# A sixteen-head attention pipeline: VectorE scales the contexts of an older unit ahead of the row maximum of the same step

## Chip, cores and metric

The kernel runs on one core of one Trainium2 chip. The metric is the device time in microseconds. Lines such as L1484 are lines of the kernel before. The engines are called TensorE (PE; PEld for its weight loads), VectorE (DVE), ScalarE (ACT), GpSimd (POOL) and SyncE (SP).

## What is computed

Twelve residual blocks on eight sequences of 256 tokens with 128 features. Three of them hold the attention that the change touches: one causal attention (block L1) and two mixtures of two attentions (block L3), all with 16 heads of 8 features. Cut to that:

```
def _L1_attn_ref(x, w_qkv, b_qkv, w_out, b_out):          # causal, 16 heads of 8
    qkv = jnp.einsum('btc,cd->btd', x, w_qkv) + b_qkv
    ...
    scores = jnp.einsum('bhqd,bhkd->bhqk', q, k) * scale
    scores = jnp.where(causal, scores, jnp.finfo(scores.dtype).min)
    attn = jax.nn.softmax(scores, axis=-1)
    out = jnp.einsum('bhqk,bhkd->bhqd', attn, v)
    return jnp.einsum('btc,cd->btd', out, w_out) + b_out

def _L3_ffn_ref(...):                                     # M = 2 attentions, mixed by mha_probs
    scores = jnp.einsum('mbhtk,mbhsk->mbhts', q, kk) / jnp.sqrt(jnp.float32(KD))
    attn = jax.nn.softmax(scores, axis=-1)
    ctx = jnp.einsum('mbhts,mbhsk->mbthk', attn, v)
    mha_out = jnp.einsum('mbthk,mhkd->mbtd', ctx, mha_wo) + mha_bo[:, None, None, :]
    x = x + jnp.einsum('mbtd,bm->btd', mha_out, mha_probs)
    ...

x = x + _L1_attn_ref(_layernorm(x, axis=-1), ...)
...
x = x + 0.5 * _L3_ffn_ref(x, ...)
x = x + _L3_attn_ref(x, ...)
x = x + 0.5 * _L3_ffn_ref(x, ...)
```

## The kernel before

Each engine has its own program, and the programs meet only in semaphores. The class SmallHeads is the pipeline of a sixteen-head attention. Its unit of work is one sequence with one set of weights: 8 units in the causal attention (the subclass L1Attend), 16 in each of the two L3 attentions (two sets of weights for each of eight sequences).

All engines walk the same list of steps, 16 to a unit: step i of unit k scores head i of unit k. Older units are further on in the same steps, so that one pass of 16 steps works on several units at once. For unit k, the one being scored:

- TensorE writes the scores of a head into one of three banks (`score_bank`, banks 0, 1 and 5 in turn), so the scores of step s wait for the row maximum of step s-3 (`topped`, `s - 2`).
- VectorE takes the row maximum of the scores (L1484; in the causal attention L1482, two masked halves with an accumulator read each) and raises `topped`.
- At step 0 GpSimd splits the 16 maxima of unit k-1 into bf16 parts (L1522 to L1528, `mx_split`) and then the projections of unit k+2 (L1536 to L1543, as long as there is a unit k+2). At step 3 TensorE turns the parts of the maxima (`mx_turned`), ScalarE copies them and SyncE sends them to the rows beside q.
- At odd steps TensorE scores a pair of heads of an older unit anew, with the maximum subtracted in the product, and ScalarE takes the exponentials (L1455). In the causal attention GpSimd then clears what lies above the diagonal (L1515, `selected`).
- Every fourth step is a quad: TensorE multiplies the exponentials of four heads with the values, which carry a column of ones, so that contexts and row sums come out together in bank 6. For w counted in quads, the causal attention waits for the select of pair 2w+1. At step 8 of unit k that is the pair scored at step 3.
- Unit k-3 is finished in bank 7, which five operations share in turn: at step 5 TensorE turns the raw contexts (L1351, `turned`), VectorE takes the reciprocal of the row sums (L1490) and scales the contexts (L1493, `scaled`). At step 7 TensorE writes the value projection of unit k into the same bank, so it waits for `scaled`, and ScalarE copies the values (L1667, L2237, `v_copied`). At step 9 TensorE turns the scaled contexts (L1365), for which it waits for `v_copied`, and ScalarE copies these (L1671, L2242).

TensorE's program has, in step 5, the four transposes L1351 first and the scores of step 5 behind them. The steps go on after the last unit has been scored, so units k-3 are scaled for k = 3 to units+2.

Of the kernel before, what the change touches and what calls it, by code (L numbers as in the profile page):

```python
# [9 lines left out]
ALU = mybir.AluOpType  # L10
# [3 lines left out]
P = 128  # L14
# [17 lines left out]
HEADS, KD = 16, P // 16  # L32
# [1173 lines left out]
class SmallHeads(Stage):  # L1206
# [264 lines left out]
    def heads_vector(self, eng, ch):  # L1471
        ps, V = self.k.ps, self.k.nc.vector
        for s, k, i in self.steps():
            if self.is_unit(k):
                self.wait_ge(eng, self.scored, s + 1)
                if i == 0:
                    self.wait_ge(eng, self.mx_split, k - 1)
                at = self.PAIRS * (i % 2) + i // 2
                mx = self.mx[k % 2][:, :, at:at + 1]
                if self.causal:  # L1480
                    for t, (st, end) in enumerate(((0, P), (P, 3 * P))):
                        o = V.tensor_tensor_reduce(self.masked[:, s % 3, st:end], ps[:, self.score_bank(s), st:end], self.k.mask_q[:, st:end], 1.0, MASKED, ALU.add, ALU.max, mx[:, t])  # L1482
                else:
                    o = V.tensor_reduce(mx, ps[:, self.score_bank(s), :].rearrange("p (t s) -> p t s", t=2), AXX, ALU.max)  # L1484
                o.then_inc(self.topped.sem, 1)
            u = k - 3
            if i == 5 and self.is_unit(u):
                self.wait_ge(eng, self.turned, u + 1)
                rows = ps[:, 7, :].rearrange("p (a d) -> p a d", d=32)[:, :, 0:2 * (KD + 1)].rearrange("p a (j d) -> p a j d", j=2)
                ch.did(V.reciprocal(self.rinv, rows[:, :, :, KD]))  # L1490
                ch.wait_ge()
                self.wait_ge(eng, self.turned_again, u)
                V.tensor_tensor(self.ctx.rearrange("p (a j d) -> p a j d", j=2, d=KD), rows[:, :, :, 0:KD],  # L1493
                                self.rinv.unsqueeze(3).to_broadcast([P, HEADS, 2, KD]), ALU.mult).then_inc(self.scaled.sem, 1)
            if i == 11 and self.ends_batch(u):
                self.wait_ge(eng, self.summed, u // self.members + 1)
                self.out_vector(u // self.members)
            c = self.norm_at(s, self.NORM_FINISHES)
            if c is not None:
                self.wait_overlaid(eng)  # L1500
                self.next.norm.finish(eng, ch, c)
# [1151 lines left out]
```

## Time and profile before

| | |
|---|---|
| median of 3 runs | 2002.47 us (1995.29 to 2004.57) |
| profiled execution, first to last instruction | 2003.0 us |
| causal attention (8 units) | about 1000 to 1130 us |
| first L3 attention (16 units) | about 1354 to 1595 us |
| second L3 attention (16 units) | about 1710 to 1950 us |

The profiled execution is one more run; its span of 2003.0 us holds all its instructions, and the three runs lie around it. In the span TensorE is busy 1685.2 us, VectorE 1299.4, ScalarE 1153.5 and GpSimd 579.3. In the middle of an L3 attention a unit takes 13.0 us (14.1 where it ends a sequence); in the causal one 13.0.

### The profile page before, as it was taken

The page shows a single profiled execution, that of the slowest core. Times are in us where ns is not written, and L with a number is a line of the kernel's source. Part 1 is how long each engine was busy: PE and PEld are TensorE (multiplying, and loading weights), DVE is VectorE, ACT ScalarE, POOL GpSimd, SP SyncE. Part 2 cuts the span into 40 slices and gives each one's busy share as a digit, 9 for nine tenths or more (in the row PEclk, how much of TensorE's full clock was granted, in tenths as well). Part 3 has the DMA queues.
Part 4 walks back from the last instruction along what each step waited for, and adds up shares of the span by engine and source line. Part 5 has one row for each costly group of instructions (what it writes and reads, how often), then busy time and mean ns, then how long its engine had stood idle before and what let it go on. Part 6 is the DMA issues. An engine that isn't in the chain of part 4 may idle for free.

```text
span 2003.0 us, 36848 instructions
## 1 busy us (share of the span) xinstructions
PE 1685.2 (84%) x13664; PEld 884.9 (44%) x13664; DVE 1299.4 (65%) x2611; ACT 1153.5 (58%) x2711; POOL 579.3 (29%) x727
## 2 busy tenths in 40 slices
PE   6897889798898889889688884978999877899986
PEld 2555345543455435553244332324555352355535
DVE  4875577545776577744577277637788464788856
ACT  3665455544455546555356664564888735488872
POOL 2552145301554045410265103313232001333200
PEclk9999999999899999989879897996999988699997
DMA  4000000000000000000252000015544000544401
GB/s 183 17 18 7 1 17 17 12 1 1 17 12 17 1 11 18 17 1 0 46 105 52 1 1 0 0 25 101 101 94 85 17 28 16 109 97 91 94 3 63
DMA packets 55016, 75.01 MB, mean 37 GB/s; under 512 B 5748, under 2 KB 38740, under 8 KB 54328
## 3 DMA queue, kind: packets, MB, share of 16 engines
q1 hardware_dynamic: 54840, 72.66, 16.0%
q8 instruction: 111, 1.82, 0.4%
q14 instruction: 65, 0.53, 0.1%
HBM read 46.39 MB, written 16.88 MB: 32 GB/s over the span
## 4 chain that ended last, share of the span: by engine, by line
PE 62%; DVE 13%; ACT 11%; issue 7%; POOL 4%; DMA 2%; SPq 0%; DVEq 0%; POOLq 0%; ACTq 0%
PE ps L195 58%; ACT arena L631 4%; DVE arena L1484 3%; PE ps L521 2%; ACT arena L1455 2%; DVE arena L702 2%; DVE arena L746 2%; ACT arena L268 1%; ACT arena L270 1%; PE ps L616 1%; PE ps L1365 1%; DVE arena L1493 1%; DMA arena<-arena 1%; DVE arena L721 1%; DMA arena<-scratch 1%
## 5 line engine op out<-in xcount | busy, mean ns | idle before, releaser
L195 PE MATMUL ps<-arena 32*64 32x128 f32 (+10 forms) x10152 | 705.0, 316 | 88.7 <-ACT arena L1455 25.5
L195 PEld LDWEIGHTS ps<-arena 32*64 32x64 f32 (+6 forms) x10152 | 397.7, 127 | 390.3 <-issue 124.5
L1455 ACT ACTIVATE arena<-ps 128x512 f32<-128x512 f32 (+1 forms) x640 | 333.8, 576 | 79.2 <-PE ps L195 70.4
L1484 DVE TENSOR_REDUCE arena<-ps 128x2 f32<-128x512 f32 x512 | 322.6, 685 | 87.2 <-PE ps L195 85.3
L195 PE MATMUL ps<-arena,w_L0f 128*128 128x512 f32 (+3 forms) x800 | 328.2, 542 | 16.9 <-DVEq L2488 9.3
L631 ACT ACTIVATE arena<-ps,arena 128x128 f32<-128x128 f32 x512 | 226.2, 460 | 136.0 <-DVE arena L748 136.0
L195 PE MATMUL ps<-arena,const 128*128 128x512 f32 (+1 forms) x536 | 186.1, 653 | 70.9 <-DVE arena L1966 22.1
L195 PEld LDWEIGHTS ps<-arena,w_L0f 128*128 128x128 f32 (+2 forms) x800 | 142.0, 192 | 142.4 <-issue 102.8
L828 POOL TENSOR_TENSOR arena<-arena 128x512 f32<-128x512 f32 x128 | 133.0, 1045 | 244.4 <-DVE arena L726 244.4
L702 DVE TENSOR_TENSOR arena<-ps,arena 128x1024 f32<-128x1024 f32 x128 | 152.4, 1205 | 10.0 <-PE ps L195 7.3
L642 ACT ACTIVATE arena<-ps 128x512 f32<-128x512 f32 x128 | 76.8, 600 | 94.4 <-DVE arena L702 91.7
L195 PEld LDWEIGHTS ps<-arena,const 128*128 128x128 f32 (+1 forms) x536 | 59.0, 161 | 158.2 <-issue 89.8
L820 POOL TENSOR_TENSOR arena<-arena 128x512 f32<-128x512 f32 x64 | 81.4, 1271 | 160.2 <-DVE arena L702 157.2
L746 DVE TENSOR_REDUCE arena<-ps 128x8 f32<-128x1024 f32 x64 | 78.3, 1223 | 63.7 <-PE ps L195 63.4
L721 DVE COPY arena<-ps 128x512 f32<-128x512 f32 x128 | 88.3, 689 | 47.7 <-PE ps L521 47.7
L631 ACT ACTIVATION_READ_ACCUMULATOR arena<-ps,arena 128x1 f32 x512 | 106.5, 208 | 0.0
L521 PE MATMUL ps<-const,arena 128*128 128x128 f32 x512 | 79.1, 277 | 30.2 <-issue 23.2
L1482 DVE CUSTOM_DVE_ANT_0 arena<-ps,masks_b 128x128 bf16<-128x128 f32 (+1 forms) x256 | 75.0, 354 | 36.2 <-PE ps L195 35.8
L521 PEld LDWEIGHTS ps<-const,arena 128*128 128x128 f32 x512 | 57.1, 141 | 93.2 <-issue 91.3
L1522 POOL CAST arena<-arena 128x32 bf16<-128x32 f32 x40 | 8.4, 209 | 280.0 <-DVE arena L1484 275.7
L821 POOL TENSOR_TENSOR arena<-arena 128x512 f32<-128x512 f32 x64 | 83.5, 1305 | 0.0
L195 PE MATMUL ps<-residual,const 128*128 128x512 f32 x96 | 56.9, 694 | 31.4 <-DVEq L2488 17.9
(227 smaller groups left out, 2134.2 us busy)
## 6 DMA issues: line engine op xcount, KB each, us to landing
scratch<-arena SPq DMA_DIRECT2D x40, 384.0 KB, 2.8
arena<-scratch SPq DMA_DIRECT2D x80, 192.0 KB
arena<-scratch SPq DMA_DIRECT2D x80, 128.0 KB
arena<-arena SPq DMA_DIRECT2D x64, 128.0 KB, 2.3
arena<-scratch SPq DMA_DIRECT2D x80, 88.0 KB
arena<-in_experts SPq DMA_DIRECT2D x16, 256.0 KB, 4.4
w_L0f<-in_L0f SPq DMA_DIRECT2D x2, 1557.0 KB, 12.2
arena<-arena SPq DMA_DIRECT2D x80, 12.0 KB
```

The source lines that it names most:

```text
L195: return self.nc.tensor.matmul(o, lhsT, rhs, start=start, stop=stop, skip_group_check=True)
L521: o = k.nc.tensor.transpose(k.ps[:, 6, (2 * j + t) * P:(2 * j + t + 1) * P], self.prob[G % 2][:, 2 * p + j, t, :], k.K("ident"))
L631: o = S.activation(self.prob[G % 2][:, j, t, :], k.ps[:, j, t * P:(t + 1) * P], ACT.Exp, bias=self.negm[G % 2][:, at:at + 1], scale=rn[:, ...
L642: self.k.nc.scalar.activation(self.sq[i], self.k.ps[:, self.block_bank(n), :], ACT.Square).then_inc(self.squared.sem, 1)
L702: self.k.nc.vector.tensor_tensor(prod.rearrange("p t (b s) -> p t b s", b=PER), x, tab, ALU.mult).then_inc(self.rotated.sem, 1)
L721: self.k.nc.vector.tensor_copy(self.probT[q % 4].rearrange("p j t s -> p (j t s)"), self.k.ps[:, 6, :]).then_inc(self.turn_copied.sem, 1)
L746: ch.did(V.tensor_reduce(self.mx[G % 2], ps[:, 0:4, 0:SEQ].rearrange("p j (t s) -> p j t s", t=2), AXX, ALU.max))
L820: G.tensor_tensor(y[:, i, :], first[:, 0, :], second[:, 1, :], ALU.add).then_inc(self.placed.sem, 1)
L821: G.tensor_tensor(y[:, i + 1, :], second[:, 0, :], first[:, 1, :], ALU.add).then_inc(self.placed.sem, 1)
L828: self.k.nc.gpsimd.tensor_tensor(pr, pr, rinv, ALU.mult).then_inc(self.scaled.sem, 1)
L1455: S.activation(self.pt[g % 4][:, e, 0:both], ps[:, self.shifted_bank(2 * g + e), 0:both], ACT.Exp, scale=self.scale).then_inc(self.exped.s ...
L1484: o = V.tensor_reduce(mx, ps[:, self.score_bank(s), :].rearrange("p (t s) -> p t s", t=2), AXX, ALU.max)
```

## The change

In the method of VectorE's program, the block that scales unit k-3 at step 5 stands ahead of the row maximum of step 5, not behind it. Waits and operations are the same.

```
     def heads_vector(self, eng, ch):
         ps, V = self.k.ps, self.k.nc.vector
         for s, k, i in self.steps():
+            u = k - 3
+            if i == 5 and self.is_unit(u):
+                self.wait_ge(eng, self.turned, u + 1)
+                rows = ps[:, 7, :].rearrange("p (a d) -> p a d", d=32)[:, :, 0:2 * (KD + 1)].rearrange("p a (j d) -> p a j d", j=2)
+                ch.did(V.reciprocal(self.rinv, rows[:, :, :, KD]))
+                ch.wait_ge()
+                self.wait_ge(eng, self.turned_again, u)
+                V.tensor_tensor(self.ctx.rearrange("p (a j d) -> p a j d", j=2, d=KD), rows[:, :, :, 0:KD],
+                                self.rinv.unsqueeze(3).to_broadcast([P, HEADS, 2, KD]), ALU.mult).then_inc(self.scaled.sem, 1)
             if self.is_unit(k):
                 self.wait_ge(eng, self.scored, s + 1)
...
                 o.then_inc(self.topped.sem, 1)
             u = k - 3
-            if i == 5 and self.is_unit(u):
...
             if i == 11 and self.ends_batch(u):
```

VectorE's program in an L3 attention, around the scaling of one unit (k even). A row with x5 stands for five row maxima; L1490 is the reciprocal, L1493 the scaling. Before:

```order
L1484 TENSOR_REDUCE arena<-ps 128x2 [waits mx_split,scored]
L1484 TENSOR_REDUCE arena<-ps 128x2 [waits scored] x5
L1490 RECIPROCAL arena<-ps 128x32 [waits turned]
L1493 TENSOR_TENSOR arena<-ps,arena 128x256 [waits turned_again,vector_step]
L1484 TENSOR_REDUCE arena<-ps 128x2 [waits scored] x10
```

The same place in the changed kernel, where the row maximum is L1493, the reciprocal L1478 and the scaling L1481:

```order
L1493 TENSOR_REDUCE arena<-ps 128x2 [waits mx_split,scored]
L1493 TENSOR_REDUCE arena<-ps 128x2 [waits scored] x4
L1478 RECIPROCAL arena<-ps 128x32 [waits turned]
L1481 TENSOR_TENSOR arena<-ps,arena 128x256 [waits turned_again,vector_step]
L1493 TENSOR_REDUCE arena<-ps 128x2 [waits scored] x11
```

One maximum, that of step 5, has moved from ahead of the reciprocal to behind the scaling. The causal attention is the same, with four instructions to a maximum. Before:

```order
1209 L1482 ISA arena<-ps,masks_b 128x128 [waits scored]
1210 L1482 ISA arena 128x1
1211 L1482 ISA arena<-ps,masks_b 128x256
1212 L1482 ISA arena 128x1
1213 L1490 RECIPROCAL arena<-ps 128x32 [waits turned]
1214 L1493 TENSOR_TENSOR arena<-ps,arena 128x256 [waits turned_again,vector_step]
```

And in the changed kernel (maximum L1491):

```order
1209 L1478 RECIPROCAL arena<-ps 128x32 [waits turned]
1210 L1481 TENSOR_TENSOR arena<-ps,arena 128x256 [waits turned_again,vector_step]
1211 L1491 ISA arena<-ps,masks_b 128x128 [waits scored]
1212 L1491 ISA arena 128x1
1213 L1491 ISA arena<-ps,masks_b 128x256
1214 L1491 ISA arena 128x1
```

The four instructions of the maximum of step 5 now follow the scaling. The order on the other engines is unchanged.

## Rows read from the trace of the kernel before

**Rows 1.** The page, part 1: busy time, share, instructions.

```profile
PE 1685.2 (84%) x13664; PEld 884.9 (44%) x13664; DVE 1299.4 (65%) x2611; ACT 1153.5 (58%) x2711; POOL 579.3 (29%) x727
```

**Rows 2.** Who waits for the scaling, L1493: us in total, times.

```profile
L1493 DVE TENSOR_TENSOR arena<-ps,arena x40: 424/424/426, 1038.6 to 1947.1; 128x256 f32<-128x256 f32 x40
...
  PE ps L195: 15.5, 31
```

**Rows 3.** Groups, TensorE, 1390 to 1570: busy, mean ns | idle before.

```profile
L195 PE MATMUL ps<-w_L3m,arena 128*128 128x128 f32 x52 | 8.9, 293 | 4.3 <-DVE arena L1493 4.3
```

**Rows 4.** Timeline, TensorE, causal attention: start, us, what [idle before].

```profile
1049.67 0.66 PE L1351 MATMUL ps<-const,arena 128*128 128x128 f32 x4
...
1052.15 0.68 PE L195 MATMUL ps<-w_L1a,arena 128*128 128x128 f32 x4 [1.38 <-DVE arena L1493]
```

**Rows 5.** Timeline, TensorE, an L3 unit.

```profile
1453.46 0.63 PE L1351 MATMUL ps<-const,arena 128*128 128x128 f32 x4
1454.02 1.72 PE L195 MATMUL ps<-arena 48*128 48x256 bf16 x24
1456.06 0.68 PE L195 MATMUL ps<-w_L3m,arena 128*128 128x128 f32 x4 [0.33 <-DVE arena L1493]
1456.68 0.62 PE L195 MATMUL ps<-arena 48*128 48x256 bf16 x8
```

**Rows 6.** Timeline, VectorE, the same L3 unit.

```profile
1452.54 2.66 DVE L1484 TENSOR_REDUCE arena<-ps 128x2 f32<-128x512 f32 x4
1455.11 0.35 DVE L1490 RECIPROCAL arena<-ps 128x32 f32<-128x32 f32 x1
1455.49 0.42 DVE L1493 TENSOR_TENSOR arena<-ps,arena 128x256 f32<-128x256 f32 x1
```

**Rows 7.** The chain that ended last, there: start, us, what.

```profile
1453.31 1.18 DVE arena L1484 x2
...
1455.93 0.14 issue
1456.06 1.23 PE ps L195 x12
...
1460.89 5.51 PE ps L195 x63
```

**Rows 8.** Timeline, TensorE, an earlier L3 unit, steps 13 to 0.

```profile
1433.69 2.14 PE L195 MATMUL ps<-arena 51*128 51x256 bf16 x28 [0.45 <-ACT arena L1455]
1435.76 1.13 PE L195 MATMUL ps<-arena,w_L3m 128*128 128x256 f32 x4
```

**Rows 9.** Timeline, ScalarE, the L3 unit: the copy of the values.

```profile
1456.78 0.49 ACT L2237 ACTIVATE arena<-ps,probs 128x256 f32<-128x256 f32 x1 [1.07 <-PE ps L195]
```

**Rows 10.** Timeline, VectorE, causal attention: maxima of steps 4 and 5.

```profile
1049.96 0.08 DVE L1482 DVE_READ_ACCUMULATOR2_ANT arena<- 128x1 f32 x1
1050.63 0.29 DVE L1482 CUSTOM_DVE_ANT_0 arena<-ps,masks_b 128x128 bf16<-128x128 f32 x1 [0.58 <-PE ps L195]
```

**Rows 11.** Timeline, the last unit of the causal attention.

```profile
1126.97 0.60 PE L1351 MATMUL ps<-const,arena 128*128 128x128 f32 x4
...
1127.61 0.36 DVE L1490 RECIPROCAL arena<-ps 128x32 f32<-128x32 f32 x1 [2.94 <-PE ps L1351]
```

**Rows 12.** Timeline, causal attention, k = 4: selects, and weights of a quad.

```profile
1051.74 1.82 POOL L1515 TENSOR_SCALAR_AFFINE_SELECT arena<-arena 128x512 f32<-128x512 f32 x3
...
1053.20 0.56 PEld L195 LDWEIGHTS ps<-arena 128*18 128x18 f32 x16 [0.16 <-issue]
```

**Rows 13.** Windows: busy PE, PEld, DVE, ACT, POOL, clock, DMA share, GB/s.

```profile
1092.40:1106.10 13.70, 12.52 (x110) 5.41 (x99) 5.33 (x35) 7.31 (x17) 5.32 (x11) 0.50 0.01 4
```

**Rows 14.** Timeline, TensorE, causal attention: turning the parts of the maxima.

```profile
1074.16 0.29 PE L195 MATMUL ps<-ident_b,arena 128*48 128x128 bf16 x2 [1.33 <-POOL arena L1528]
...
1087.08 0.29 PE L195 MATMUL ps<-ident_b,arena 128*48 128x128 bf16 x2 [1.32 <-POOL arena L1528]
...
1102.51 0.41 PE L195 MATMUL ps<-ident_b,arena 128*48 128x128 bf16 x2 [0.96 <-POOL arena L1528]
```

More of the change, by code:

```diff
@@ L1486, in heads_vector @@
             u = k - 3
-            if i == 5 and self.is_unit(u):
[L1488 to L1494, printed above, removed]
             if i == 11 and self.ends_batch(u):
```

## The prediction

> **What bounds the kernel now.** I read the page first, for the engines. TensorE is busy 84% of the span, VectorE 65%, ScalarE 58% [rows 1]. No stage-independent bound follows from such averages, so I went to the two operations that the change moves. The next view is the one of the context scaling itself (L1493, 40 of them): who waits for it. TensorE does, 31 times, 15.5 us in all [rows 2]. That number is the whole prize that a step on VectorE alone can win, and the 31 is telling: the change alters the order only where a unit k is still being scored while unit k-3 is scaled, that is for k = 3 to units-1. That makes 5 places in the one causal attention (8 units) and 13 in each of the two L3 attentions (16 units), 31 together. The other 9 scalings of the 40 stand in steps without a row maximum and stay where they are.
>
> The 31 waits are of two kinds. In the first L3 attention the value matmuls (four matmul records a unit, 52 for 13 units) stood idle 4.3 us behind L1493, 0.33 us each [rows 3]; the second has the same number of places, and 26 x 0.33 us is 8.6 us. What is left, 6.9 us, is the causal attention's five, 1.38 us each [rows 4].
>
> One L3 unit in the timeline shows why. TensorE turns the raw contexts at 1453.46 to 1454.09, goes on with the scores of steps 5 and 6 and the quad of step 6 until 1455.74, and then stands until 1456.06 before the value projection of step 7, which overwrites bank 7 and so must wait for the scaling [rows 5]. VectorE meanwhile works without a pause: the four maxima of steps 2 to 5 in one run from 1452.54, the reciprocal at 1455.11, the scaling from 1455.49 to 1455.91 [rows 6]. The chain of waits says that this is the path that sets the end: maxima of steps 3 and 4 (1453.31 to 1454.49), the maximum of step 5, reciprocal, scaling, 0.14 us of issue, then 1.23 us of TensorE's twelve matmuls [rows 7].
>
> **The change, part by part.** It adds and removes no instruction. Per place, VectorE's reciprocal and scaling change places with the maximum of step 5. The turned contexts are always there first, because TensorE's queue has the four transposes ahead of the scores of step 5. So the wait that moves holds the maximum for nothing that its own scores were not behind anyway, and no other queue's order changes.
>
> L3, 26 places. The maximum of step 4 ends at 1454.49 [rows 7] and the transposes at 1454.09 [rows 5], so the reciprocal can start at about 1454.51 in place of 1455.11: 0.60 us earlier. The scaling then ends at 1455.31, and with the 0.14 us of issue [rows 7] TensorE may go on at 1455.45. It is busy until 1455.74 anyway. The whole gap closes and VectorE has 0.29 us to spare. What that gives is 0.33 us by the row; a little more, since work that is not held starts shortly before the modelled end of its predecessor (1433.69 + 2.14 is 1435.83, and the next starts at 1435.76, which is 0.07 us before it [rows 8]). I take 0.39 us, from the same seam behind the value matmuls [rows 5] (1456.06 + 0.68 against a next start of 1456.68), and keep 0.33 as the lower bound: 26 x 0.39 = 10.1 us, at least 8.6 us.
>
> Does the gain travel? What follows hangs on the value matmuls: ScalarE's copy of the values stood idle 1.07 us for them [rows 9], so it moves with them, then the second turning, the exponentials and the 5.51 us of TensorE work behind them [rows 7]. I see no wait in this chain on anything that does not start from TensorE. TensorE is the engine with least room there, and its pause is what goes.
>
> Causal attention, 5 places. Here VectorE is idle, not late. It ends the maximum of step 4 at 1050.04 and waits 0.58 us for the scores of step 5 [rows 10], while the turned contexts are there at 1050.33 [rows 4]. VectorE follows a transpose within 0.04 us (L1351 from 1126.97 for 0.60, L1490 at 1127.61 [rows 11]). So the reciprocal starts at about 1050.37 in place of 1051.19, and all behind it is 0.82 us earlier: the value projection at 1051.33 in place of 1052.15.
>
> For k = 6 and 7 this 0.82 us passes on: 2 x 0.82 = 1.6 us. For k = 3, 4 and 5 it does not. GpSimd there still splits projections of later units and comes to the three selects of steps 1, 3 and 5 only at 1051.74, 1.82 us for the three; the quad of step 8 needs the second, which ends at about 1052.97. Its weights are loaded at 1053.20 now [rows 12], so at most some 0.17 us is left to win: 3 x 0.17 = 0.5 us. Between the ends of this term, 0 and 0.82 us each, I take the select's time, since the quad waits for that select by name.
>
> Sum: 10.1 + 1.6 + 0.5 = 12.2 us, with bounds of 8.6 (L3 by the bare row, nothing of the causal one) and 15.5 plus the seams, 17. The profiled execution spans 2003.0 us and the median of three runs is 2002.47 (1995.29 to 2004.57), 0.5 lower. So 2003.0 - 12.2 = 1990.8 by the profile, 1990.3 by the median; I say 1990.5 us.
>
> What does it cost? The maximum of step 5 ends later, by reciprocal and scaling. In L3 it would run from about 1455.23 to 1455.91; the maximum of step 6 is where it was. TensorE asks for the maximum of step 5 at the scores of step 8, because score banks come round every third step. Those are the last two of the twelve matmuls that end at 1457.29 [rows 7], so about 1457.1 now and 1456.7 then. That leaves 0.8 us, which is what hides this edit. GpSimd's split of the maxima comes ten steps later.
>
> The skill has a rule against the change. The Trainium skill, Perfetto Trace Analysis, Identifying the Most-Contended Engine, says that improving a kernel generally means improving the engine with the highest occupancy. By it a new order on VectorE, which lowers no engine's busy time, would leave 2002.5 us. That is rival 2.
>
> **Rivals.** (1) The pause on TensorE partly turns into another wait. For it: later in each unit TensorE waits for ScalarE's exponentials (0.45 us at 1433.69 [rows 8]), and moving the value copy does not shorten ScalarE's work. Against it: ScalarE's idle 1.07 us ahead of the copy [rows 9]. If L3 keeps only a third (3 us) and the causal one gives nothing, 1999.5 us; half of each, 1996.4.
>
> (2) Nothing comes of it: the wait moves whole to the next hand-over, 2002.5 us. In the rows that would need a second path as long as the first, within 0.3 us, in all units. For that speaks only that VectorE has few pauses in L3; against it, that its maximum of step 8 waited for TensorE.
>
> (3) TensorE's clock. In the causal attention it is granted half its clock, the 1.2 GHz level, for the 13.7 us from 1092.4 [rows 13], after two pauses, of 1.32 us ahead of 1087.08 [rows 14] and of 1.38 us at the scaling of k = 7 (the size of [rows 4]). The turning of the maxima comes every 12.92 us at full speed (1074.16 to 1087.08), and the next took 15.43 us (to 1102.51) [rows 14]: 2.5 us a unit. Two of the removed pauses lie right ahead of this. If the fall is spared, 2.5 to 5 us more come back: 1985.5 to 1988. If one such stretch is added instead, 1993. The Trainium skill, TensorE: Matmul & The Clock Gate, says in its part on the gate that the default state is throttled and that activity releases it, which points to the first; but pauses of the same size earlier in this stage cost no clock in this trace.
>
> (4) Slower. The late maximum of step 5 holds the scores of step 8. It decides once TensorE comes to them before the maximum's end, 0.8 us earlier than I think. If all of the 0.72 us of reciprocal and scaling (0.38 + 0.34) fell on TensorE at 31 places, 22.3 us would be lost against 12.2 won: 2012.5 us. Against it stands the 0.8 us just worked out.
>
> **How the numbers follow.** Forecast 0.55, with a range of its own of 1988 to 1993; rival 1 0.20; rival 2 0.08; rival 3 0.13, of which 0.10 on the fast side; rival 4 0.04. About 0.5% (10 us, so 1992.5) is what a measurement of this kernel can tell from no change, and the forecast lies only 2 us beyond it: I put 0.49 of its 0.55 there. Faster: 0.49 + 0.10 = 0.59. Slower: rival 4, 0.04. The rest, 0.37, is within 0.5%. The range, 1986 to 2000, holds the forecast, most of rival 1 and the clock's cases, and leaves out rivals 2 and 4.
>
> **What would show it.** In the profile after: no wait of TensorE for the scaling in the L3 attentions; L3 units 0.39 us shorter; in the causal one, waits of about 0.57 us at five places in place of 1.38, a wait for the select of L1515 at the quads of step 8 for k = 3 to 5, and only in k = 6 and 7 a unit shorter by 0.8. The maximum of step 5 starts right behind the scaling. The prediction is wrong if TensorE's idle time behind ScalarE's exponentials or VectorE's maxima grows by what the scaling gives back, or if the clock falls in another place.

## The result

Five runs of each kernel on one chip gave 1983.95 us (1977.95 to 1990.05) for the changed kernel and 2002.47 us (1995.29 to 2007.0) for the one before: ratio 0.9909, 95% interval 0.9882 to 0.9936. It is faster by over 0.5%, as forecast, but by 18.5 us where 12.2 were worked out, and just outside the range (1986 to 2000). With later runs of the same two kernels added they lie nearer together: 23 runs of the change have a median of 1987.34 us, 78 of the kernel before a median of 1999.25, 11.9 us apart (means 1986.53 and 1999.86, 13.3 apart). The experiments below ask which of the two differences belongs to the change.

The profiled execution of the changed kernel spans 1982.2 us, 20.8 less than that of before. Its profile has the same busy times to within 1%; TensorE's is 11.2 us lower [rows 1]:

```profile
PE 1674.0 (84%) x13664; PEld 882.1 (45%) x13664; DVE 1300.0 (66%) x2611; ACT 1152.3 (58%) x2711; POOL 578.9 (29%) x727
```

Who waits for the scaling, now L1481 (us in total, times), answers to [rows 2]:

```profile
L1481 DVE TENSOR_TENSOR arena<-ps,arena x40: 423/425/426, 1038.7 to 1925.2; 128x256 f32<-128x256 f32 x40
...
  PE ps L195: 2.7, 5
```

Of 31 waits of TensorE five are left, all in the causal attention, 0.54 us each in the mean where they were 1.38. In the groups of TensorE (1380 to 1556) the value matmuls of L3, idle 4.3 us in [rows 3], show no wait:

```profile
L195 PE MATMUL ps<-w_L3m,arena 128*128 128x128 f32 x52 | 9.3, 300 | 0.0
```

The timeline of TensorE in an L3 unit answers to [rows 5]:

```profile
1455.21 1.72 PE L195 MATMUL ps<-arena 48*128 48x256 bf16 x24
1456.86 0.71 PE L195 MATMUL ps<-w_L3m,arena 128*128 128x128 f32 x4
1457.50 0.62 PE L195 MATMUL ps<-arena 48*128 48x256 bf16 x8
```

1455.21 + 1.72 is 1456.93: the value projection starts 0.07 us before the modelled end of the quad, where it started 0.32 us after it. VectorE's timeline there [rows 6]:

```profile
1452.52 3.26 DVE L1493 TENSOR_REDUCE arena<-ps 128x2 f32<-128x512 f32 x5 [0.91 <-PE ps L195]
1455.70 0.35 DVE L1478 RECIPROCAL arena<-ps 128x32 f32<-128x32 f32 x1
1456.08 0.42 DVE L1481 TENSOR_TENSOR arena<-ps,arena 128x256 f32<-128x256 f32 x1
1456.42 1.28 DVE L1493 TENSOR_REDUCE arena<-ps 128x2 f32<-128x512 f32 x2
```

Five maxima ahead of the reciprocal (steps 0 to 4), two behind the scaling. The scaling ends at 1456.50, 0.36 us ahead of the value projection. The chain of waits [rows 7] no longer touches VectorE in these units:

```profile
1458.24 0.41 PE ps L1365 x2
...
1462.05 0.59 ACT arena L1455
...
1462.68 5.72 PE ps L195 x68
1468.40 0.59 PE ps L1351 x4
1468.99 2.84 PE ps L195 x35
...
1471.96 0.41 PE ps L1365 x2
```

From one turning of the scaled contexts (L1365) to the next is a unit; 1458.24 to 1471.96 is 13.72 us, and the unit before it was 12.75. In the causal attention the chain goes another way, through GpSimd:

```profile
1049.46 1.17 POOL arena L1540
...
1051.38 1.15 POOL arena L1544
1052.53 1.19 POOL arena L1516 x2
...
1053.76 0.84 PE ps L195 x16
1054.61 0.38 PE ps L1365 x2
```

These are the last three operations of the split of a later unit's projections (L1540, L1542, L1544; the middle one is left out above), two selects, then the sixteen matmul records of the quad of step 8. TensorE waits for the select there three times, 1.7 us in all, as the prediction had it for k = 3 to 5.

### The profile page after: what moved, and what is told of

Its sections match the earlier page's. It is cut to its first block, busy times and chain, and to the rows that moved or that the text cites. A ratio compares the mean times of both kernels' runs of the same rounds, so it can differ in the third digit from the quotient of the medians.

```text
span 1982.2 us, 36848 instructions
## 1 busy us (share of the span) xinstructions
PE 1674.0 (84%) x13664; PEld 882.1 (45%) x13664; DVE 1300.0 (66%) x2611; ACT 1152.3 (58%) x2711; POOL 578.9 (29%) x727
## 4 chain that ended last, share of the span: by engine, by line
PE 64%; ACT 12%; DVE 10%; issue 7%; POOL 4%; DMA 2%; SPq 0%; DVEq 0%; POOLq 0%; ACTq 0%
PE ps L195 59%; ACT arena L631 5%; PE ps L521 2%; ACT arena L1455 2%; DVE arena L702 2%; DVE arena L746 2%; ACT arena L268 1%; DMA arena<-scratch 1%; PE ps L1351 1%; ACT arena L270 1%; PE ps L616 1%; PE ps L1365 1%; DVE arena L809 1%; DVE arena L721 1%; ACT arena L263 1%
## 5 line engine op out<-in xcount | busy, mean ns | idle before, releaser
L1493 DVE TENSOR_REDUCE arena<-ps 128x2 f32<-128x512 f32 x512 | 322.6, 685 | 76.9 <-PE ps L195 74.8
L195 PEld LDWEIGHTS ps<-arena,w_L0f 128*128 128x128 f32 (+2 forms) x800 | 140.2, 190 | 140.9 <-issue 98.6
L1491 DVE CUSTOM_DVE_ANT_0 arena<-ps,masks_b 128x128 bf16<-128x128 f32 (+1 forms) x256 | 74.5, 353 | 30.3 <-PE ps L195 29.7
## 6 DMA issues: line engine op xcount, KB each, us to landing
w_L0f<-in_L0f SPq DMA_DIRECT2D x2, 1557.0 KB, 12.2
```

The lines of the kernel that those rows point to most:

```text
L195: return self.nc.tensor.matmul(o, lhsT, rhs, start=start, stop=stop, skip_group_check=True)
```

## The experiments

Stage lengths read best from the starts of L1365 and of the operation that opens the stage (L1607 of before). The table sets side by side all profiles of the two kernels (us): causal attention from its opening to its last L1365; in it units 3 to 6; each L3 attention from its first to its last L1365 (15 units, 12 of them changed); and the stretch between the last L1365 of the first L3 attention and the opening of the second, in which the change moves nothing.

| profile | causal | units 3 to 6 | L3, first | between | L3, second |
|---|---|---|---|---|---|
| before | 145.2 | 38.94 | 190.5 | 116.8 | 190.4 |
| before again | 138.3 | 38.93 | 190.4 | 117.7 | 190.4 |
| before, third | 143.5 | 40.28 | 190.5 | 116.7 | 190.4 |
| change | 137.6 | 37.75 | 186.0 | 113.1 | 186.0 |
| change again | 139.0 | 37.74 | 186.0 | 113.1 | 185.9 |
| change, third | 138.9 | 37.74 | 186.0 | 115.5 | 186.0 |

The L3 attentions are the clean comparison, since TensorE's granted clock is full there in both kernels. The windows of the first one, before and after (busy PE, PEld, DVE, ACT, POOL; clock; DMA share; GB/s):

```profile
1403.16:1593.63 190.47, 175.36 (x2000) 91.74 (x2001) 138.51 (x238) 154.27 (x306) 47.15 (x92) 1.00 0.36 73
1392.71:1578.75 186.04, 174.88 (x2000) 91.75 (x2000) 138.49 (x238) 154.27 (x306) 47.17 (x92) 1.00 0.38 76
```

The work is the same to within 0.5 us of TensorE's modelled time, and the attention is 4.43 us shorter.

**One part of the change alone.** In heads_vector, the block ahead of the maximum is taken only where the attention is not causal (first kernel) or only where it is (second); elsewhere it stays behind it:

```
+            if i == 5 and self.is_unit(u) and not self.causal:      # L3 alone; "and self.causal" in the second
...
+            if i == 5 and self.is_unit(u) and not (not self.causal):   # behind the maximum
```

Expected of L3 alone: 

> The new order in the two L3 attentions alone, the old one in the causal attention. Theory A (the order gives what it gives at its 31 places, the rest of the 18 us is TensorE's clock, which falls elsewhere from run to run): about 8.6 us faster than before (26 places x 0.33), ratio about 0.996; in the profile, two L3 units take 26.47 us from L1365 to L1365 as in the change (27.13 before), and the causal attention is as long as before within what its clock makes. Theory B (the causal attention's new order saves its clock, each time): the same 8.6 us here, and the causal attention keeps a half-clock stretch of some 13 us. Theory C (the L3 stages give more than their 26 pauses): over 12 us faster.

Measured: 1990.05 us against 1998.43, ratio 0.9946 (0.9922 to 0.9970). Both L3 attentions take 186.0 us, the causal one 139.0 with units 3 to 6 in 38.93.

Expected of the causal attention alone: 

> The new order in the causal attention alone. Theory A: about 2.1 us faster than before (2 x 0.8 + 3 x 0.17), which the timed runs cannot tell from nothing, ratio 0.999; units of 12.83 us for k = 3 to 5, held by the select of L1515, as in the change. Theory B: 7 to 10 us faster, ratio about 0.996, because less of the causal attention runs at half clock. Theory C: as A.

Measured: 1998.93 us against 1998.43, ratio 0.9998 (0.9977 to 1.0020). L3 took 190.5 and 190.4 us; units 3 to 6 of the causal attention 37.74, but the next unit 15.09, at half clock, and the stage 138.9 in all. So nearly everything that can be timed is in L3, and theory B falls: a gain of 7 us from the causal attention is outside the interval, and the half clock came there with the new order too. That the new order spares it now and then is not excluded by the stage's length alone: with the old order it took 145.2, 138.3, 143.5 and 139.0 us, and with the block ahead of the maximum of step 3, 4 or 5 and the splits at step 0, in eight profiles, 135.5 to 140.2. Theory C falls too, since L3 gives 4.4 us an attention over 12 changed units, 0.37 us each, and no more.

**The same kernels again.** No edit. Expected of the change again: 

> The changed kernel once more, for a second profile and five more times. Theory A: the ratio comes out between 0.990 and 0.997, nearer to 0.9945 (11 us) than the first time, and the half-clock stretches of the causal attention and of the stages that the change does not touch lie in other places than in the first profile. Theory B: the causal attention again has at most two short half-clock stretches (3.4 us each) before its last two units. Theory C: the ratio again about 0.991, and the surplus stands in the L3 stages.

Measured: 1989.64 us against 1998.43, ratio 0.9955 (0.9935 to 0.9976). That is theory A's; 0.991 is outside the interval, and the L3 stages took what they took the first time.

Expected of the kernel before again: 

> The kernel before once more, one look, for a second profile of it. Theory A: its causal attention's half-clock stretches need not be those of the first profile (13.7 us from 1092.4), and stage by stage it differs from the first profile by a few us where nothing is changed. Theory B: the 13.7 us at half clock from about k = 7 on are there again.

Measured, one run: 1998.51 us. Its causal attention took 138.3 us, 6.9 less than in the first profile of the same kernel. The windows of the stage show why (busy PE, PEld, DVE, ACT, POOL; clock; DMA share; GB/s). The first profile of before:

```profile
983.30:1128.50 145.20, 110.99 (x1167) 55.91 (x1167) 83.80 (x536) 75.49 (x176) 72.94 (x126) 0.79 0.35 71
```

The second, the same 1167 matmul records at a mean granted clock of 0.84 of full:

```profile
981.20:1119.50 138.30, 103.74 (x1167) 53.72 (x1167) 83.85 (x536) 75.09 (x176) 72.37 (x125) 0.84 0.37 74
```

TensorE's busy time falls by 7.25 us, VectorE's stays. In this second profile the clock is full from 1040 us to the end of the stage. The half clock of [rows 13] was the first execution's, not the kernel's.

Expected of the third time: 

> The changed kernel a third time. Theory A: ratio near 0.9945 again, between 0.992 and 0.997; L3 units 12.67 and 13.72 us exactly as in the two profiles so far; the stage between the two L3 attentions takes 113.1, 116.7 or 117.7 us by how long after the first L3 attention the half clock sets in, and the causal attention 137.6 to 139 us. Theory B (the first ratio, 0.9909, is the true one): 0.991 again.

Measured: 1984.39 us against 2000.13, ratio 0.9922 (0.9900 to 0.9945). This interval holds 0.991 as well as 0.9941, so it does not decide between the theories by itself. The L3 units were the same again; the stretch between the L3 attentions took 115.5 us, none of the three lengths expected.

Expected of before, third: 

> The kernel before a third time, one look. Theory A: the causal attention takes 138 to 145 us by where its clock falls, L3 units 13.05 and 14.08 us as in both profiles so far, and a half clock that sets in 6.5 us after the first L3 attention goes with a following stage of 113.1 us here too, since that has nothing to do with the change.

Measured, one run: 1996.1 us, with 143.5 us in the causal attention and the L3 units as before. The half clock set in 7.4 us behind the first L3 attention, with 116.7 us between. That 6.5 us goes with 113.1 us for the old kernel too could therefore not be seen.

**What holds the causal attention at k = 3 to 5.** First, GpSimd's splits later, for units 3 to 7 there:

```
-            if i == (2 if u == 2 else 0) and self.is_unit(u):
+            if i == (6 if self.causal and u > 2 else 2 if u == 2 else 0) and self.is_unit(u):
```

Expected: 

> The changed kernel, and in the causal attention GpSimd's splits of the projections of unit k+2 (3.6 us) stand at step 6, behind the selects of steps 1, 3 and 5, not at step 0. Theory A says that these splits alone hold back the gain of the causal attention at k = 3 to 5: then the unit from L1365 to L1365 falls from 12.83 us to about 12.2 (0.65 less), as it is from k = 6 on (12.1), some 2 us in all, and TensorE waits no more for L1515 at step 8. Rival: another wait (the maxima of steps 9 to 14, or the select of step 7 for the quad of step 12, which now stands behind the splits) holds the unit at 12.8 or more. The timed ratio to before then stays about 0.995 by either.

Measured: 1998.02 us against 1999.73, ratio 0.9993 (0.9968 to 1.0018). The three units that have splits take 16.4, 17.3 and 17.0 us, but at a mean granted clock of 0.79, 0.70 and 0.64, so that only a part of this is the waits'. GpSimd's timeline:

```profile
1044.69 1.16 POOL L1544 TENSOR_TENSOR arena<-arena 128x512 bf16<-128x512 f32 x1
1045.80 1.82 POOL L1516 TENSOR_SCALAR_AFFINE_SELECT arena<-arena 128x512 f32<-128x512 f32 x3
```

The selects are behind the splits as before, now the ones that the quad of step 12 needs, and TensorE's waits for them (1030 to 1095) became longer than those of the change (1.7 us in all):

```profile
PE ps L195 <- POOL arena L1516: 4.8, 3, 1.7
```

The rival was right as to the wait, and the edit did not answer the question. So the work itself was cut in the next kernel, in which units 3 to 7 of the causal attention do not get the low parts of q and k:

```
+                if self.causal and u > 2:
+                    G.tensor_tensor(self.rest, qk, self.part(0), ALU.subtract).then_inc(self.low.sem, 1)
+                    continue
```

Expected: 

> The changed kernel without the last two operations of GpSimd's split (L1542 and L1544 there, 1.8 us) for units 3 to 7 of the causal attention; their low parts of q and k are then not computed. Theory A (GpSimd's splits hold the gain back at k = 3 to 5): the selects come 1.8 us sooner, TensorE's wait for them at step 8 is gone, and the unit falls from 12.83 to about 12.1 to 12.2 us. Rival (something else holds the unit, the selects only look like it): it stays at 12.8.

Measured, one run: 1988.52 us. The units after k = 3 and 4 take 12.19 us each, 0.64 less than in the change. (The next, at half clock in part, took 13.52.) The chain there:

```profile
1046.59 1.60 PE ps L195 x25
1048.18 0.60 PE ps L1351 x4
1048.81 0.37 DVE arena L1478
1049.20 0.44 DVE arena L1481
1049.64 0.14 issue
1049.77 1.90 PE ps L195 x26
```

No select between: transposes, reciprocal, scaling, value projection, as the prediction had it for k = 6 and 7. GpSimd's splits are what takes 0.64 of the 0.82 us away at k = 3 to 5 (13.01 us a unit before, 12.83 in the change, 12.19 here).

**How late a maximum may be.** The same block one and two steps earlier:

```
-            if i == 5 and self.is_unit(u):
+            if i == 4 and self.is_unit(u):        # second kernel: i == 3
```

Expected at step 4: 

> The changed kernel with the scaling one step earlier still, ahead of the maximum of step 4, so that VectorE waits for the turning of the raw contexts with two maxima behind it. It doubles what my rival 4 feared, a late maximum. By the slack I worked out (the scores of step 7 ask for the maximum of step 4 some 0.7 us after it ends) the L3 units stay at 12.67 and 13.72 us and the causal ones at 12.83, ratio 0.995. By rival 4 TensorE waits for the maximum of step 4 or 5 at steps 7 and 8, the L3 unit grows by up to 0.7 us, and the kernel is up to 20 us slower than the change.

Measured: 1988.96 us against 1999.73, ratio 0.9939 (0.9913 to 0.9965). L3 takes 186.0 us twice, as in the change, and in 1390 to 1570 TensorE waits on nothing but exponentials:

```profile
PE ps L195 <- ACT arena L1455: 7.6, 17, 0.6
```

In the causal attention it is not quite free: the unit of k = 6 takes 12.32 us where the change has 12.09.

Expected at step 3: 

> The changed kernel with the scaling ahead of the maximum of step 3, to find the point from which the late maximum decides (rival 4). TensorE's scores of step 6 ask for the maximum of step 3 and stand ahead of the value projection. In L3 VectorE reaches the scaling early, waits for the transposes of step 5 and ends the maximum of step 3 some 0.8 to 0.9 us after TensorE wants it. If my reading of the slack is right (0.7 us and more at steps 4 and 5, none at 3), the L3 unit grows by 0.3 to 0.9 us against the change, 8 to 25 us in all, ratio to before 1.000 to 1.008. If late maxima are hidden in general, it stays at 12.67 and the ratio at 0.9945.

Measured: 2015.19 us against 2000.13, ratio 1.0088 (1.0056 to 1.0119). L3 units grow by 1.25 us (13.92 from 12.67), more than the upper end expected. TensorE's wait for the maximum is 0.97 us of it. Most of the rest is the seam: the 24 matmuls behind the transposes, 1.72 us in one piece in the change, are cut in two by the wait and take 0.61 and 1.38 us in the timeline. Its waits, 1390 to 1570, and the chain of a unit:

```profile
PE ps L195 <- DVE arena L1493: 12.6, 13, 1.0
```

```profile
1447.55 0.60 PE ps L1351 x4
...
1448.18 0.37 DVE arena L1478
...
1448.57 0.42 DVE arena L1481
1448.99 0.61 DVE arena L1493
...
1449.65 2.57 PE ps L195 x30
```

Now the maximum of step 3 is on the path behind the scaling. Rival 4 is a real mechanism and the change stands two steps away from it.

**The next wait in L3.** ScalarE copies the raw contexts one step later, behind the exponentials of step 11:

```
-            w = self.quad_at(s)
+            w = self.quad_at(s if self.causal else s - 1)
```

Expected: 

> The changed kernel, and in the L3 attentions ScalarE copies the raw contexts (L1461, 0.60 us) behind the exponentials of step 11, not ahead of them. It asks which wait is next on the path after the change: the chain names ScalarE's exponential ahead of TensorE's pair of step 13, 0.45 us of idle time a unit. If that wait is next and nothing takes its place, L3 units get 0.3 to 0.45 us shorter (12.3 us), 8 to 12 us in all, ratio to before about 0.990. Rival: the quad of step 14, which waits for the copy, takes over the wait, and the units stay at 12.67.

Measured: 2006.68 us against 1999.73, ratio 1.0022 (0.9998 to 1.0046), and 193.2 us for each L3 attention, 7.2 more than in the change. The chain:

```profile
1464.93 3.40 PE ps L195 x35
...
1468.80 0.59 ACT arena L1455
1469.39 0.50 ACT arena L1461
1469.89 0.14 issue
1470.03 5.18 PE ps L195 x62
```

The pair of step 13 is still held by an exponential, and the quad of step 14 by the copy. Both waits are paid where one was: the unit takes 13.18 us, neither the 12.3 hoped for nor the rival's 12.67.

Expected of the last two edits together: 

> The last two edits together on top of the change: the splits of the causal attention at step 6, and the raw copy behind the exponentials of step 11 in L3. If both work, their gains add, since they lie in different stages: some 2 + 10 us below the change, ratio to before about 0.989. If the second does not work, about 0.994.

Measured: 2018.53 us against 1999.73, ratio 1.0079 (1.0054 to 1.0104): the losses of both parts, not gains. No version tried beats the change; the one at step 4 is not to be told from it.

## Why the prediction came out as it did

**L3, 26 places: right.** "The whole gap closes": the wait is gone in all 26. The step of 0.39 us a place measured 0.37, so 9.6 us for 10.1. The seam taken from a neighbouring row was the right idea and a little too large, the bare 0.33 would have been low. "Does the gain travel?": it does, unit after unit, in each of the seven profiles with the block ahead of the maximum of step 5 or 4 in L3 and the raw copy at its old place.

**Causal attention: right, and its split too.** 0.82 us for k = 6 and about 0.17 for k = 3 to 5: units 3 to 6 together fell by 1.19 us (38.93 to 37.74) where 2 x 0.17 + 0.82 is 1.16. The units of 12.83 us are the select's, and the cut split shows the cause. For k = 7 the profiles of the change were at half clock in part; the one with the later raw copy was not: 12.10 us, where the kernel before has 12.92 in its second profile.

**The cover of the late maximum: right.** In L3 it holds at step 4 as well and is gone at step 3.

**What failed** is the last step, "The range, 1986 to 2000", with the base it stands on and the term for the clock. "2003.0 - 12.2 = 1990.8 by the profile, 1990.3 by the median" takes one profile and three runs as the kernel's time. (The profile's span is not even the same measure: in the runs that list both, the timed value is 1.7 to 1.9 us above the span.) Runs of the same kernel lie from 1990.77 to 2011.5 us, those of the change from 1977.95 to 1995.74: each spreads over some 20 us, more than the effect. Of the 6.6 us between the forecast of 1990.5 and the 1983.95 measured, 3.2 are this base (2002.47, where 78 runs have 1999.25) and 3.4 the five runs of the change (1983.95, where 23 have 1987.34). The lower end of the range, 1986, lies only 1.3 us under the median of the 23, and 11 of them are below it. The range had no term for this spread: rival 3 let the clock move only in the causal attention. The profiles show it moving the stages that the change does not touch as well. Between the L3 attentions the change's profile has (busy PE, PEld, DVE, ACT, POOL; clock):

```profile
1578.75:1691.83 113.08, 76.61 (x234) 44.53 (x235) 66.53 (x137) 53.24 (x87) 10.15 (x18) 0.89 0.12 33
```

and the kernel with the new order in L3 alone, whose code there is the same:

```profile
1583.51:1701.26 117.75, 83.17 (x237) 46.22 (x237) 66.65 (x137) 53.57 (x87) 10.10 (x18) 0.84 0.12 31
```

TensorE is busy 6.6 us longer at the lower clock, and the stretch is 4.7 us longer. Of the 20.8 us between the first two profiles, 9.6 + 2.2 us are the order's; of the other 9, some 5 are the first profile's half clock in the causal attention and 3.7 this stretch. The stretches that are left differ by up to 2 us either way and about cancel. By the timed runs the order's 11.8 us lie beside 11.9 (medians) or 13.3 us (means, standard error 1.2) of all runs. The 18.5 us of the first five runs are the order's gain and a favourable draw.

That the draw goes with TensorE's clock can be seen in the timed runs too, because a mean granted clock is on record for all 23 runs of the change and for 73 of the 78 before. Within either kernel a run is the longer the lower this clock (correlation -0.92 and -0.93), by some 1.5 us for each 0.001. The run that is the median of the first five had 0.935, the 23 have 0.932 in the mean, which by that slope is 4.5 us. The change does not raise the clock: the 73 runs before have 0.933. So rival 3's spared clock is not what the change gives on average. But at equal clock the two kernels lie 14.2 us apart (a line fitted to both, standard error 0.5; at 0.932, for instance, 1986.7 us over five runs and 1999.9 over twelve). That is 2.4 us more than the 11.8 that the profiles place, and where these 2.4 us arise stays open.

The forecast's sign and gain were right for the kernels' long-run medians (a ratio of 0.994, forecast and measured); its time was 3.2 us too high for them, by the base, and its range too narrow on the low side. The rule that the prediction set against the change (the Trainium skill, Perfetto Trace Analysis, Identifying the Most-Contended Engine), read as "no busy time falls, so nothing is won", is not borne out: in the L3 windows above busy times stayed within 0.5 us and 4.43 us were won. What the change shortened was the idle time of the engine with the highest occupancy.

## What to carry to other kernels

Look for the operation that the busiest engine waits for, and for what stands ahead of it in its own engine's program without need: moving two small operations past one of 0.7 us, where the work they wait for was long done, gave 0.37 us a unit, the whole pause and the seam, though no engine had less to do. Bound the gain by the pause, not by how much earlier the operation comes, ask which queue the engine meets next (here GpSimd's, which left 0.17 of 0.82 us), and find from the ring of buffers how late the operation that was passed may be. Take a range's width from the spread of the unchanged kernel's own runs; with three of them, it is wider than it looks.

## What was not expected of the hardware

Two executions of the same instructions can differ by several us in one stage, with TensorE's clock. After the first L3 attention the granted clock falls to the 1.2 GHz level in every one of the fourteen profiles, at different moments. Where that came 6.4 to 6.6 us after the last L1365, the stretch to the next attention took 113.1, 113.1 and 113.2 us (the change, the change again, the later splits); at 5.4 us 117.7, 117.8 and 117.7 (before again, L3 alone, step 4); at 7.4 us 116.8, 116.7 and 116.6 (before, before third, causal alone). The other five do not make it a rule: 116.7 at 4.7 us (the later raw copy), 116.6 at 4.6 (both edits), 114.1 at 4.2 (step 3), 115.5 at 5.6 (the change, third) and 115.8 at 6.3 (the cut split). The instructions of the stretch are the same in all of them. No experiment moved the fall by itself, so that its moment sets the length is a guess from the nine that agree.
